# Two fused layers: the last residual sum of twelve units as an accumulating transfer instead of a GpSimd addition

## The reference, cut to what matters

```
x = x + layernorm(attn(layernorm(x)))
      attn: decaying prefix sum along the sequence, gelu, W_proj, + its own input, layernorm with gamma, beta
x = x + layernorm(ffn(layernorm(x)))
      ffn:  sigmoid(xr W_r) * (relu(xk W_k)^2 W_v),  xr, xk: mixes of a token and the one before it
```

## Time and profile before

| | us |
|---|---|
| median of three runs | 165.47 |
| profiled execution | 164.04 |
| its span | 162.3 |
| TensorE busy | 135.9 (84%) |
| ScalarE busy | 134.3 (83%) |
| VectorE busy | 131.9 (81%) |
| GpSimd busy | 131.6 (81%) |

### The profile page before, as it was taken

How to read it: one execution, slowest core, us unless ns; L and a number is a source line. 1 busy time by engine, 2 the same in 40 slices (tenths; PEclk the granted TensorE clock), 3 DMA queues, 4 the chain that set the end, 5 groups by cost and what they waited for, 6 DMA issues and landing times.

```text
span 162.3 us, 3207 instructions
## 1 busy us (share of the span) xinstructions
PE 135.9 (84%) x913; PEld 115.0 (71%) x913; DVE 131.9 (81%) x365; ACT 134.3 (83%) x395; POOL 131.6 (81%) x199
## 2 busy tenths in 40 slices
PE   0157895996899996999999999999999999999500
PEld 0055784895587966979879788799788778777500
DVE  0968999999999999999999989899998499730600
ACT  4357999878979895998999489989969979899970
POOL 4358899889898917498899979879988899989893
PEclk9999999599999999999999999999999999999965
DMA  3699900000000000000002020020402002222606
GB/s 103 153 272 330 275 2 2 4 0 2 0 0 4 0 0 2 6 0 0 0 0 69 0 65 2 4 69 0 129 0 69 0 0 67 69 65 65 194 1 193
DMA packets 18672, 8.98 MB, mean 55 GB/s; under 512 B 1504, under 2 KB 18656, under 8 KB 18656
## 3 DMA queue, kind: packets, MB, share of 16 engines
q1 hardware_dynamic: 18224, 8.79, 18.4%
q10 hardware_dynamic: 432, 0.00, 0.1%
HBM read 4.59 MB, written 4.19 MB: 54 GB/s over the span
## 4 chain that ended last, share of the span: by engine, by line
PE 62%; DVE 24%; POOL 5%; issue 3%; ACT 2%; ACTq 1%; POOLq 1%; DVEq 0%
PE ps_v L641 8%; PE ps_prefix L584 7%; PE ps_r L632 7%; PE ps_r L631 7%; PE ps_k L620 7%; PE ps_k L621 7%; PE ps_z L599 6%; DVE x_raw L391 4%; PE ps_prefix L586 4%; DVE ps_z L448 3%; PE ps_tT L611 3%; PE ps_xT L577 3%; DVE conv_scaled L426 3%; PE ps_z L600 3%; DVE conv L432 2%
## 5 line engine op out<-in xcount | busy, mean ns | idle before, releaser
L288 ACT ACTIVATE xn<-x_all,x_bias,x_r 128x128 f32<-128x128 f32 x64 | 26.2, 485 | 5.9 <-POOL x_bias L187 3.8
L344 ACT ACTIVATE f_normal<-f,out_bias,f_r 128x128 f32<-128x128 f32 x64 | 26.1, 485 | 1.5 <-POOL out_bias L237 1.5
L632 PE MATMUL ps_r<-mixed_T,tsT 128*128 128x128 f32 x128 | 24.7, 275 | 0.0
L631 PE MATMUL ps_r<-mixed_T,tsT 128*128 128x128 f32 x128 | 24.7, 275 | 0.0
L584 PE MATMUL ps_prefix<-prefix_ones,xn_pow 128*128 128x256 f32 x64 | 21.4, 418 | 3.8 <-DVE conv_scaled L426 3.6
L194 POOL TENSOR_TENSOR xn_pow<-xn,pow_token 128x512 f32<-128x512 f32 x16 | 20.3, 1271 | 2.4 <-ACT xn L288 2.4
L599 PE MATMUL ps_z<-pv_T,gelu 128*128 128x128 f32 x128 | 22.1, 277 | 0.0
L631 PEld LDWEIGHTS ps_r<-mixed_T,tsT 128*128 128x128 f32 x128 | 19.8, 192 | 2.4 <-issue 2.4
L249 POOL TENSOR_TENSOR x_all<-x_all,f_normal 128x512 f32<-128x512 f32 x16 | 20.1, 1273 | 0.0
L308 ACT ACTIVATE junk<-ps_z 128x128 f32<-128x128 f32 x64 | 16.8, 280 | 4.0 <-PE ps_z L600 3.7
L599 PEld LDWEIGHTS ps_z<-pv_T,gelu 128*128 128x128 f32 x128 | 19.5, 192 | 0.4 <-issue 0.4
(11 more groups left out here) (85 smaller groups left out, 347.5 us busy)
## 6 DMA issues: line engine op xcount, KB each, us to landing
out_x<-x_all SPq DMA_DIRECT2D x16, 256.0 KB, 2.2
x_all<-in_x SPq DMA_DIRECT2D x7, 512.0 KB, 5.9
x_all<-in_x SPq DMA_DIRECT2D x2, 256.0 KB, 3.6
w_pv<-in_W_proj SPq DMA_DIRECT2D x1, 64.0 KB, 4.6
w_pv<-in_W_v SPq DMA_DIRECT2D x1, 64.0 KB, 4.4
w_rk<-in_W_r SPq DMA_DIRECT2D x1, 64.0 KB, 5.0
w_rk<-in_W_k SPq DMA_DIRECT2D x1, 64.0 KB, 4.1
gamma_row<-in_gamma SPq DMA_DIRECT2D x1, 64.0 KB, 3.0
```

Of the source, the lines that this page charges most:

```text
L288: last = a_.activation(tile(xn[u % D], j), xa(u, j), ACT.Identity, bias=col(x_bias, u, j), scale=col(x_r, u, j))
L344: last = a_.activation(tile(f_normal[u % D], j), tile(f[u % D], j), ACT.Identity, bias=col(out_bias, u, j), scale=col(f_r, u, j))
L631: t_.matmul(tile(ps_r, j), tsT[u % D][:, q, l + 1:l + 1 + P], mixed_T[:, 0, :], start=True, stop=False)
L632: last = t_.matmul(tile(ps_r, j), tsT[u % D][:, q, l:l + P], mixed_T[:, 1, :], start=False, stop=True)
```

## The change

For units 0 to 11 `add_f` becomes a transfer that GpSimd issues: it reads `f_normal` and adds it to `x_all` in SBUF. A transfer can add but not subtract here, so `f` keeps its sign: `keep_pv` no longer negates, and `out_bias` becomes minus the sum of the two means instead of their difference, which takes one more small instruction on GpSimd in each `f_scale_of`. Units 12 to 15 keep the GpSimd instruction, now as an addition. Each of the twelve transfers has a semaphore of its own, `out_summed[u]`; the store of unit u and `scale_f` of unit u + 4 wait for it.

```diff
+SUM_BY_DMA = 12
@@ SyncE, stores
             for u in range(UNITS):
-                sp.wait_ge(out_ready, u + 1)
+                if u < SUM_BY_DMA:
+                    sp.wait_ge(out_summed[u], 16)
+                else:
+                    sp.wait_ge(out_ready, u - SUM_BY_DMA + 1)
@@ GpSimd, f_scale_of
-                g_.tensor_tensor(cols(out_bias, u, n), cols(y_mean_r, u, n), cols(f_mean_r, u, n),
-                                 ALU.subtract).then_inc(f_scale, n)
+                g_.tensor_tensor(cols(f_sum, u, n), cols(y_mean_r, u, n), cols(f_mean_r, u, n),
+                                 ALU.add).then_inc(f_sum_done, n)
+                pool.wait_ge(f_sum_done, u + n)
+                g_.tensor_scalar(cols(out_bias, u, n), cols(f_sum, u, n), -1.0, 0.0, ALU.mult, ALU.add).then_inc(f_scale, n)
@@ GpSimd, add_f
                 pool.wait_ge(f_scaled, u + 1)
-                g_.tensor_tensor(xa(u, 0, TILES), xa(u, 0, TILES), f_normal[u % D][:], ALU.subtract).then_inc(out_ready, 1)
+                if u < SUM_BY_DMA:
+                    g_.dma_start(xa(u, 0, TILES), f_normal[u % D][:], accum_op=ALU.add).then_inc(out_summed[u], 16)
+                else:
+                    g_.tensor_tensor(xa(u, 0, TILES), xa(u, 0, TILES), f_normal[u % D][:], ALU.add).then_inc(out_ready, 1)
@@ ScalarE, scale_f
-                after(act, out_ready, u - D + 1)
+                if 0 <= u - D < SUM_BY_DMA:
+                    act.wait_ge(out_summed[u - D], 16)
+                else:
+                    after(act, out_ready, u - D - SUM_BY_DMA + 1)
@@ VectorE, keep_pv
-                v_.tensor_copy(pv_T[:, 0, :], tile(ps_k, 0))
-                v_.tensor_scalar(pv_T[:, 1, :], tile(ps_k, 1), -1.0, None, ALU.mult).then_inc(s_pv_ready, 1)
+                v_.tensor_copy(pv_T[:].rearrange("p w c -> p (w c)"), ps_k[:, 0:2 * P]).then_inc(s_pv_ready, 1)
```

More of the change, by code:

```diff
@@ L77, in sandwich @@
         t_ve, t_r = sb("t_ve", UNITS * TILES), sb("t_r", UNITS * TILES)
-        f_ve, f_r, f_mean_r, out_bias = (sb(n, UNITS * TILES) for n in ("f_ve", "f_r", "f_mean_r", "out_bias"))
+        f_ve, f_r, f_mean_r, f_sum, out_bias = (sb(n, UNITS * TILES) for n in (
+            "f_ve", "f_r", "f_mean_r", "f_sum", "out_bias"))
         ps_xT, ps_prefix, ps_z0, ps_z1, ps_tT, ps_k, ps_r, ps_v = (
@@ L107, in sandwich @@
             "f_ready", "f_stats", "f_ve_done", "f_r_done", "f_mean_done", "f_scale"))
-        f_scaled, out_ready, stored = sem("f_scaled"), sem("out_ready"), sem("stored")
+        f_scaled, f_sum_done, out_ready, stored = (sem(n) for n in ("f_scaled", "f_sum_done", "out_ready", "stored"))
+        out_summed = [sem(f"out_summed{u}") for u in range(SUM_BY_DMA)]
         block = ctx.enter_context(nc.Block())
```

## The result

In 20 runs each, the changed kernel took 165.92 us (165.25 to 166.76) and the kernel before 164.20 us (164.07 to 165.56). The ratio is 1.0085, with a 95% interval of 1.0065 to 1.0105: slower, by about 1.4 us. Both kernels take one of two levels about 1.1 us apart (before mostly 164.1, sometimes 165.3; after 165.45 or 166.45), the upper one in ten of twenty runs after, six of twenty before and all three ahead of the prediction, so the medians lie 1.72 us apart and like levels 1.2 to 1.3. The two profiled executions are both of the lower level, 164.04 and 165.25 us, with spans of 162.3 and 163.4, so their traces can be laid side by side.

What follows compares the result with a forecast made beforehand. TensorE was taken to set the pace, with GpSimd just keeping up. 164.04 - 0.06 + 0.35 + 1.8 = 166.13 us, so +2.09; on the median of 165.47 that gave 167.56, stated as 167.5, range 165.2 to 173.0.

Steps and rivals of the forecast that it cites:

- 10c - 10.2: GpSimd's lateness at unit 15's scale, from ten issues and the longer biases, less 0.42 in hand: 1.8 us.
- The bound: From 84 to 152 us TensorE is busy 68.00 of 68.00 us; GpSimd just keeps up, so lightening it gains nothing.
- keep_pv: One copy of 256 columns replaces two instructions of 0.19 and 0.20 us: 0.33 us taken, so -0.06 us.
- The issue, c: GpSimd's time to issue one transfer, replacing a subtraction of 1.235 us: 1.2 us, between 0.43 and 1.98.
- The extra bias instruction: One more dependent step per bias on GpSimd: 0.37 us for a pair, 0.35 for one unit, ten times.
- One lateness, in series: Idle of TensorE near 140 us and delay in the last 15 us are one 1.8 us, not added twice.
- Where it reaches the others: Unit 14's t_r through ScalarE's t_scaled to TensorE's transpose, 0.83 us in hand: about 0.5 us idle near 140 us.
- The transfer's own time: L, issue to landing: 4 us taken, between 2.2 and 7.2; up to 5.5 before scale_f(12) waits, so no cost.
- Dear issue: Rival: an issue costs GpSimd 1.6 us or more, lateness 5.8 us and more, 171.6 us upward; chance 0.13.
- lands late: Rival: at a landing time of 7 us scale_f(12) waits 1.5 us, 1.3 us is paid, 167.1 us; chance 0.06.
- faster: Rival: GpSimd holds the timed runs up by 1.43 us, cheaper issues give it back, 164.3 us; chance 0.09.
- Keeps up: Rival: with c at or below 1.02 GpSimd has no lateness; +0.29 remains, 165.76 us; chance 0.30.

Runs made afterwards that it cites:

- the doubled one: The changed kernel with a second accumulating transfer, into a scratch tensor, issued ahead of each of the twelve: 174.45 us, ratio 1.0616 against the kernel before.
- the sign elsewhere: The changed kernel, transfers kept, with the mean of y negated behind y_ve and out_bias one subtraction again: 164.15 us, ratio 1.0004 against the kernel before.

## Why the prediction was right in kind and wrong in size

The step that failed is the lateness of GpSimd's list, 10c - 10.2 = 1.8 us at c = 1.2. The runs showed 0.86 us. Its size was wrong, since an issue took 1.07 us. Its form was wrong too, since what counts is the largest lateness on the way and not the one at the end: at c = 1.07 the same sum gives +0.8 us in all, while the two profiled executions differ by 1.21. A second error is the base, 165.47 us, the median of three runs, where that of twenty is 164.20.

- *The bound.* Right: TensorE is full, GpSimd has nothing in hand, and relief gains nothing. The kernel without sums shows it directly.
- *keep_pv.* One copy took 0.33 us of the chain, as taken (an interpolation that happened to hit):

```profile
16.48 0.33 DVE pv_T L497
```

- *The issue, c.* This is the step that failed in size. I took 1.2 us, the middle of 0.43 and 1.98. Between fixed neighbours it is 1.06 for a pair. The same reading gives savings of 0.00 us (unit 2), 0.34 (3 and 4, with a wait of 0.34 for f_normal in it), 0.09 (5), 0.20 (6), 0.29 (7), 0.36 (8 and 9) and 0.35 (10 and 11): 1.63 for ten issues, and so 1.07 each. With that, 10c - 10.2 is 0.5 and not 1.8 us. Two SyncE rows are a wide bracket for GpSimd, and at a slope of ten the 0.13 us of error make 1.3. The 1 us of the Trainium skill ("DMA: Bandwidth & Descriptors", section Latency and other measured facts), which the sum had left aside, was nearer, though it is the time to a transfer's first byte and not what GpSimd spends.
- *The extra bias instruction.* Right in all, with errors that cancel: 2.21 us of lateness measured in the kernel with it alone, or 2.04 from where the stretch begins, against 2.15. Two of the six pairs cost 0.47 and not 0.37, and GpSimd did have something in hand that I had passed over as not a wait for another engine: 0.45 us ahead of `f_mean_r` at 108.67, of which 0.14, the usual step, is left in the changed kernel. For one unit at the end the step was 0.29, not 0.35.
- *One lateness, in series.* Wrong in form. GpSimd itself was ready at about 154.70 for unit 15 (it waited 0.29 us), 0.57 later than 154.13, which is near the 0.5 of c = 1.07, but in part by luck: the changed trace enters the stretch 0.19 us ahead (94.29 against 94.48), which the sum doesn't have. And 0.86 us was paid, since the lateness had been larger on the way (0.88 at unit 14's z scale), TensorE had turned it into a gap, and a gap in a full engine doesn't close when GpSimd catches up. The end takes the largest lateness on the way less what is in hand there, not the one at the end.
- *Where it reaches the others.* I named ScalarE's t_scaled and the transpose, with a gap of 0.5 near 140 us. The gap was 0.54 at 139.86, but by VectorE's z scale and gate(11); that it has the size and nearly the place of the forecast is luck. The way that I had named is real: it made the wait of 0.18 at unit 12's transpose, 0.58 in the kernel with the bias alone and 1.82 in the doubled one. I had measured what is in hand on one way and for one unit only.
- *The transfer's own time.* Right: 3.3 to 4.4 us landed inside 5.5, at no cost. It was close: in the kernels with the transfers alone and with the sign elsewhere single ones took up to 5.3.
- *The sum.* +2.09 forecast, +1.21 between the two profiled executions. Put on a median of three high runs it became 167.5, against 165.92 measured.
- *The rivals.* "Dear issue", "lands late" and "faster" are out by the runs above, and the 1.43 us between the timed runs and the profile, on which "faster" rested, is for the most part the distance of the two levels. "Keeps up" was nearly right about c but had no room for a peak on the way.

## What to carry to other kernels

Where one engine is full and another runs without a gap beside it, ask of an edit not what it takes off the second engine but whether it adds a dependent step to it: here one small dependent instruction cost about four times an independent one (0.37 against 0.09 us), and seven of them, 2.5 us in all, outweighed ten lighter sums, 1.6 us. Count lateness at each hand-over, less what is in hand there, and take the largest, since a gap in the full engine stays. Price a new kind of operation between two neighbours that do not change, not by its own row.

## What the runs showed of the hardware

An accumulating SBUF to SBUF transfer of 256 KB issued by GpSimd took 0.95 to 1.24 us of GpSimd's list as one among other instructions, 1.06 each as two, 0.88 for each further one in a row, and landed 3.3 to 4.4 us after its issue, up to 5.4 in the other kernels that issue it once and up to 6.7 in the doubled one. A VectorE addition with both operands in SBUF lengthened a 0.20 us GpSimd instruction to 0.56. The two levels of run time, which all but the doubled kernel showed, part long before the first sum. The profiled execution without sums is of the upper level, and up to 84 us its list is that of the kernel before. Here are two products of the first unit's prefix_sum, before and there:

```profile
16.32 0.66 PE L584 MATMUL ps_prefix<-prefix_ones,xn_pow 128*128 128x256 f32 x2
```
```profile
16.81 1.06 PE L586 MATMUL ps_prefix<-prefix_ones,xn_pow 128*128 128x256 f32 x2
```

The granted clock is 1.00 there in both. From 38 to 44 us it is 0.72 without sums and 1.00 before, and from 47 us on TensorE's list without sums is 1.2 to 1.4 us behind. The trace of the sign elsewhere (164.67 us) also has the 1.06; the other eight have 0.64 to 0.70. What sets it off is open.
